# Attention in a four-layer block: probabilities times V in pairs of heads that write opposite halves of the output partitions

## The chip, the cores and the metric

One core of a Trainium2 chip runs the whole program as one launch. The metric is the device time of one execution in microseconds (us), the median of several runs. Five engines work from queues of their own and meet at semaphores: TensorE (PE in the profile, with its weight loads as PEld), VectorE (DVE), ScalarE (ACT), GpSimd (POOL) and SyncE (SP), which issues most transfers.

## The reference, cut to what matters

The program is a block of four layers: a state-space layer, an attention network of depth 2 (attention and a gated feed-forward part, twice), a linear-attention layer and a mixture of experts. The change touches only the local attention, which runs twice (layer 0 and layer 1 below), on 8192 tokens of width 256, 8 heads of 64, windows of 128 tokens, each attending to itself and the window in front of it:

```
def local_attention(q, k, v):              # b, heads 8, n 2048, head width 64
    w = n // WINDOW                        # WINDOW = 128
    bq, bk, bv = windows of q * 8, k, v    # (b, h, w, 128, 64)
    bk, bv = (look_around(bk), look_around(bv))   # window before + own: 256 keys
    sim = jnp.einsum('bhwid,bhwjd->bhwij', bq, bk)
    sim = jnp.where(mask, -jnp.finfo(sim.dtype).max, sim)
    attn = jax.nn.softmax(sim, axis=-1)
    out = jnp.einsum('bhwij,bhwjd->bhwid', attn, bv)      # <- the changed product
    return out.reshape(b, h, n, d)
```

Queries and keys are normalised and rotated first; the output goes through a projection `wo` and is added to the layer's input. All of it is float32.

## The kernel before, in words

`attention()` builds the programs of the five engines for one layer (`made` is true for layer 0, whose queries and keys an earlier stage has already computed; layer 1 computes its own). It walks over 64 tiles of 128 tokens, one window each, and the loops of the engines are written out by hand: the order of calls in a loop is the order in the engine's queue, and semaphores (`wait_ge`, `then_inc`) order the engines among each other. The 8 heads of a tile are worked on in two halves of four, A (half 0) and B (half 1). Per tile and half:

- `scores` (L945) multiplies queries by keys into the PSUM tile `p_s`. A head has only 64 rows, so it takes one half of TensorE's rows; the inner loop over `g` issues two heads on opposite row halves one after the other.
- `maxima` on VectorE (L1151) adds the mask, writes `probA` or `probB` and, per head, the negated maximum into `nb`; ScalarE (L1055) takes the exponential; VectorE divides (`normalise`, L1134 reciprocal, L1138).
- `turn_prob` transposes the probabilities on TensorE (L962) into `p_t`; ScalarE (L1066) and VectorE (L1169) each copy half of it to `probT`.
- `weighted_values` (L975) is the product with V, into the PSUM tile `p_o`, transposed: head `h` takes 64 partitions (the lower half for even `h`, the upper half for odd `h`) and 128 columns. Its keys are two windows, `w` = 0 and 1, from `v` of the tile before and of this one, so each head is two matmuls that accumulate. It uses all 128 rows of TensorE but only 64 of its columns; the start partition of the output says which 64.
- When both halves are done, ScalarE copies `p_o` to `oT` (L1041), TensorE projects (L984), VectorE adds the residual (L1161).

Beside that, per tile, later tiles are prepared: queries and keys are rotated (VectorE L1181, L1184, L1186; GpSimd L1263), their norms are taken (ScalarE L1085, VectorE L1194 and L1196, GpSimd L1259, a power), keys are scaled (GpSimd L1274), both are transposed (TensorE L927, ScalarE L1072), and the values are computed (TensorE L913; in layer 1 also queries and keys, L905).

The order of the calls for one tile `t` of layer 0, which sets what is queued behind what:

- TensorE: scores A, transposing a later input (L895), product with V of half B of tile t-1, scores B (waits for all four maxima of half A), values, transposing A, projection of t-1, transposing the rotated queries and keys of t+1, product with V of half A, transposing B (waits for the copy `qkT` by ScalarE, since both use `p_t`).
- VectorE: maxima A, norms (L1194, L1196), normalise A, maxima B, copy A, residual of t-1 (waits for the projection), normalise B, rotation, copy B.

In layer 1 the order is: on TensorE scores A, L895, product B of t-1, scores B, projection, first part of L905, transposing A, second part, L927, L913, product A, transposing B; on VectorE copy B of t-1, maxima A, normalise A, maxima B, residual, copy A, normalise B, rotation, norms.

The product is issued head by head. `head_at(half, j)` is `4 * half + 2 * (j % 2) + j // 2`, so that `j` = 0, 1 are the two even heads of the half (lower output partitions) and `j` = 2, 3 the two odd ones (upper). A float32 matmul of the program is two MATMUL instructions in the profile, so one group of the product, the work of one half of one tile, is 16 MATMULs. There are 2 halves x 64 tiles x 2 layers = 256 groups.

Of the kernel before, what the change touches and what calls it, by code (L numbers as in the profile page):

```python
# [14 lines left out]
P = 128  # L15
# [9 lines left out]
H, DK = 8, 64  # L25
# [836 lines left out]
def attention(nc, ctx, A, rows, l, ident, identb, mhalf, qk_d, S, before):  # L862
# [7 lines left out]
    qsc, rc, rsn, qkT, vv, prob, probT, nb, den, rden, oT = (  # L870
        S.qsc, S.rc, S.rsn, S.qkT, S.vv, S.prob, S.probT, S.nb, S.den, S.rden, S.oT)
    p_qk, p_v, p_s, p_t, p_o = S.p_qk, S.p_v, S.p_s, S.p_t, S.p_o
# [13 lines left out]
    def head_at(half, j):  # L886
        return 4 * half + 2 * (j % 2) + j // 2

    def tensor(pe, then):
# [75 lines left out]
        def weighted_values(t, half):  # L965
            if half == 0:
                pe.wait_ge(s_ve, n0 + t + 1)
                if t > 0:
                    pe.wait_ge(s_xo, n0 + t)
            pe.wait_ge(s_pe[half], n0 + t + 1)  # L970
            pe.wait_ge(s_pa[half], n0 + t + 1)
            for j in range(4):
                h = head_at(half, j)
                for w, u in enumerate(((t - 1) % RING, t % RING)):
                    ins = pe.matmul(p_o[(h % 2) * DK:(h % 2 + 1) * DK, (h // 2) * P:(h // 2 + 1) * P],  # L975
                                    vv[u][:, h * DK:(h + 1) * DK], probT[:, j, w, :], start=(w == 0), stop=(w == 1),
                                    skip_group_check=True)
            ins.then_inc(s_pv[half], 1)

        def project(t, part):  # L980
# [9 lines left out]
        for t in range(-2, NT + 1):  # L990
# [7 lines left out]
            if t >= 1:  # L998
                weighted_values(t - 1, 1)
# [30 lines left out]
            if now:  # L1030
                weighted_values(t, 0)
                turn_prob(t, 1)
# [1809 lines left out]
```

## Time and profile before

| | |
|---|---|
| median of 3 runs | 5740.58 us (5739.33 to 5742.49) |
| profiled execution, first to last instruction | 5737.1 us |
| PE busy / share of the span | 5081.1 us / 89% |
| DVE | 4318.9 us / 75% |
| ACT | 2963.0 us / 52% |
| POOL | 2975.0 us / 52% |
| L975, the product with V: 4096 MATMULs | 406.0 us busy, 279 ns mean |
| L945, the scores: 4096 MATMULs | 300.7 us busy, 287 ns mean |

The profiled execution is known by its span only; the median lies 3.5 us above it, which is what lies around the first and last instruction. "Busy" is a union: where two instructions of an engine run at once, that time counts once. MATMUL ends are modelled, and each stays on record for some 0.27 us although the next can start earlier, so that an engine with short waits still shows as busy. The layers follow one another: layer 0 runs from about 1947 to 2747 us of the span, layer 1 from about 3240 to 4266 us.

### The profile page before, as it was taken

How to read it: one execution, taken by the hardware profiler on the slowest of the kernel's cores; microseconds unless marked ns; L12 is line 12 of the kernel's file. 1: busy time of each engine (PE TensorE's matmuls, PEld its weight loads, DVE VectorE, ACT ScalarE, POOL GpSimd, SP SyncE). 2: the span in 40 equal slices, each digit the busy share in tenths (PEclk: the TensorE clock that was granted, in tenths of full speed). 3: DMA queues.
4: the chain of work that ended last, by engine and by line, in shares of the span. 5: the costliest groups of instructions: out<-in, count | busy, mean ns of one | idle time of the engine just before them, and what ended most of it. 6: DMA issues, size and time to landing. Idle time of an engine off the chain costs nothing. (4 is left out here: it accounts for less than half of the span.)

```text
span 5737.1 us, 79616 instructions
## 1 busy us (share of the span) xinstructions
PE 5081.1 (89%) x26068; PEld 3035.9 (53%) x26068; DVE 4318.9 (75%) x8753; ACT 2963.0 (52%) x6267; POOL 2975.0 (52%) x1603
## 2 busy tenths in 40 slices
PE   7778777777875699999999999999999999998876
PEld 2223232223221477777655666666665556666765
DVE  3999999999999688888333577777763338994279
ACT  4776776777776477777111355555541114442232
POOL 4999899989989555555111344444431110003733
PEclk9899999989997799999999999999999999999987
DMA  5665556655655222223112111111111134445755
GB/s 134 145 153 144 136 141 153 149 135 146 150 138 120 69 89 84 87 89 95 45 55 73 35 34 34 34 34 34 45 40 55 55 113 141 149 149 137 185 157 178
DMA packets 501470, 593.79 MB, mean 103 GB/s; under 512 B 59702, under 2 KB 380996, under 8 KB 496964
## 3 DMA queue, kind: packets, MB, share of 16 engines
q1 hardware_dynamic: 486756, 579.36, 36.9%
q10 hardware_dynamic: 2016, 7.34, 0.4%
q0 software_dynamic: 12288, 2.00, 0.3%
q8 instruction: 211, 3.46, 0.3%
q14 instruction: 199, 1.63, 0.1%
HBM read 425.05 MB, written 180.37 MB: 106 GB/s over the span
## 5 line engine op out<-in xcount | busy, mean ns | idle before, releaser
L654 POOL TENSOR_TENSOR db<-durep,brep 128x2048 f32<-128x2048 f32 x256 | 1160.5, 4533 | 188.1 <-DVE p_h L561 177.3
L513 ACT ACTIVATE p_h<-dlrep,am 128x512 f32<-128x512 f32 x1024 | 704.5, 691 | 195.8 <-DVE hh L572 170.7
L561 DVE TENSOR_TENSOR_SCAN p_h<-p_h,hlast,db 128x512 f32<-128x512 f32 x576 | 719.9, 1282 | 0.0
L1259 POOL TENSOR_TENSOR rn<-n,mhalf 128x16 f32<-128x16 f32 x128 | 374.9, 2929 | 642.8 <-DVE n L1196 642.7
L349 PE MATMUL p_acc<-hh,fold 128*32 128x512 f32 x2048 | 314.6, 690 | 341.9 <-DVE hh L572 340.7
L572 DVE TENSOR_TENSOR hh<-p_h,crep 128x512 f32<-128x512 f32 x768 | 519.6, 677 | 0.0
L1263 POOL TENSOR_TENSOR rot_cos<-rot_cos,rot_sin 128x1024 f32<-128x1024 f32 x128 | 301.9, 2358 | 220.9 <-DVE rot_sin L1186 220.9
L1635 POOL TENSOR_TENSOR grstd<-grstd,mhalf 128x4 f32<-128x4 f32 x32 | 32.6, 1018 | 737.6 <-DVE grstd L1552 737.5
L975 PE MATMUL p_o<-probT,v 128*64 128x128 f32 x4096 | 406.0, 279 | 6.0 <-DVE probT L1169 3.4
L1066 ACT ACTIVATE probT<-p_t 128x512 f32<-128x512 f32 x256 | 152.8, 597 | 482.0 <-PE p_t L962 482.0
L975 PEld LDWEIGHTS p_o<-probT,v 128*64 128x64 f32 x4096 | 344.1, 137 | 90.4 <-issue 70.6
L1537 ACT ACTIVATE gg<-p_s,b 128x512 f32<-128x512 f32 x160 | 109.9, 687 | 447.4 <-PE p_o L1480 266.2
L349 PEld LDWEIGHTS p_acc<-hh,fold 128*32 128x32 f32 x2048 | 42.4, 114 | 559.9 <-DVE hh L572 535.4
L642 POOL TENSOR_TENSOR hh<-hs,crep 128x512 f32<-128x512 f32 x256 | 327.0, 1277 | 12.6 <-DVE hs L561 12.6
L945 PE MATMUL p_s<-qkT 64*128 64x128 f32 x4096 | 300.7, 287 | 15.8 <-DVE nb L1151 8.0
L1480 PE MATMUL p_s<-ghT,w 128*128 128x512 f32 x640 | 302.5, 595 | 5.2 <-DVE ghid L1589 3.6
L945 PEld LDWEIGHTS p_s<-qkT 64*128 64x128 f32 x4096 | 251.3, 189 | 68.9 <-DVE nb L1151 45.5
L1501 PE MATMUL p_t<-w,ghid 128*128 128x256 f32 x1280 | 284.8, 382 | 0.0
L561 DVE TENSOR_TENSOR_SCAN hs<-p_h,hlast,db 128x512 f32<-128x512 f32 x192 | 245.5, 1279 | 49.1 <-ACT p_h L513 46.8
L1055 ACT ACTIVATE probB<-probB,nb 128x256 f32<-128x256 f32 x512 | 253.3, 498 | 50.3 <-DVE nb L1151 50.3
L227 PE MATMUL p_f<-mxT,w_in 128*128 128x512 f32 x512 | 259.8, 654 | 8.1 <-ACT mxT L390 5.5
L502 ACT ACTIVATE hlast<-p_h 128x1 f32<-128x1 f32 x576 | 95.3, 166 | 329.9 <-DVE hh L572 328.8
(285 smaller groups left out, 11994.9 us busy)
## 6 DMA issues: line engine op xcount, KB each, us to landing
dlrep<-delta_rows SPq DMA_DIRECT2D x256, 256.0 KB
durep<-drive_rows SPq DMA_DIRECT2D x256, 256.0 KB
ew<-in_L_ffn_w SPq DMA_DIRECT2D x192, 176.0 KB
first_queries_keys<-qs SPq DMA_DIRECT2D x128, 256.0 KB, 2.1
qk<-first_queries_keys SPq DMA_DIRECT2D x64, 512.0 KB, 3.8
brep<-bc_rows SPq DMA_DIRECT2D x64, 256.0 KB
crep<-bc_rows SPq DMA_DIRECT2D x64, 256.0 KB
delta_rows<-dl SPq DMA_DIRECT2D x64, 256.0 KB
```

The lines of the kernel that those rows point to most:

```text
L349: ins = pe.matmul(p_acc[32 * j:32 * j + 32, :], fold[:], hh[s % 2][:, j], start=False, stop=(g == NG - 1), skip_group_check=True)
L513: act.activation(p_h[:, (i % BANKS) * CH:(i % BANKS + 1) * CH], dlrep[use % 2][:, j], ACT.Exp, scale=am[:, q, j, g:g + 1]).then_inc(s_ex, 1)
L561: dve.tensor_tensor_scan(out=state, data0=bank, data1=db[s % 2][:, j], initial=0.0 if first else hlast[:, i % TILES:i % TILES + 1], op0=AL ...
L572: dve.tensor_tensor(out=hh[s % 2][:, j], in0=p_h[:, (i % BANKS) * CH:(i % BANKS + 1) * CH], in1=crep[c % 2][:, s % NG], op=ALU.mult).then_ ...
L642: pool.tensor_tensor(out=hh[s % 2][:, 0], in0=hs[s % 2][:], in1=crep[c % 2][:, s % NG], op=ALU.mult).then_inc(s_hp, 1)
L654: pool.tensor_tensor(out=db[s % 2][:], in0=durep[use % 2][:], in1=brep[c % 2][:, g:g + 1, :].to_broadcast([P, 4, CH]), op=ALU.mult).then_i ...
L945: ins = pe.matmul(p_s[:, at:at + P], here[g * DK:(g + 1) * DK, c:c + P], there[g * DK:(g + 1) * DK, INNER + c:INNER + c + P], start=True, ...
L975: ins = pe.matmul(p_o[(h % 2) * DK:(h % 2 + 1) * DK, (h // 2) * P:(h // 2 + 1) * P], vv[u][:, h * DK:(h + 1) * DK], probT[:, j, w, :], sta ...
L1259: pool.tensor_tensor(out=rn[f % 2][:], in0=n2[f % 2][:], in1=mhalf[:], op=ALU.pow).then_inc(s_rn, 1)
L1263: pool.tensor_tensor(out=rc[:], in0=rc[:], in1=rsn[:], op=ALU.add).then_inc(s_rot, 1)
L1480: ins = pe.matmul(dst[:], w1[:, f, o + j * P:o + (j + 1) * P], hT[:, f, :], start=(f == 0), stop=(f == DH - 1))
L1501: ins = pe.matmul(p_y[:, j0 * D:(j0 + 1) * D], hid[:, j, j0 * P:(j0 + 1) * P], w2[:, j, :], start=False, stop=(j == FB - 1), skip_group_ch ...
```

## The change

The four heads of a group are no longer issued one after the other. The outer loop now goes over `a` (which of the two 128-column blocks of `p_o`), then over the two windows `w`, and the inner loop over `g`, the lower and the upper half of the output partitions. So a matmul for the lower half is followed by one for the upper half. The number, the shapes, the operands and the semaphores of the group stay, and so does its place in the queue.

```diff
-            for j in range(4):
-                h = head_at(half, j)
+            for a in range(2):
                 for w, u in enumerate(((t - 1) % RING, t % RING)):
-                    ins = pe.matmul(p_o[(h % 2) * DK:(h % 2 + 1) * DK, (h // 2) * P:(h // 2 + 1) * P],
-                                    vv[u][:, h * DK:(h + 1) * DK], probT[:, j, w, :], start=(w == 0), stop=(w == 1),
-                                    skip_group_check=True)
+                    for g in range(2):
+                        j, h = 2 * g + a, 4 * half + 2 * a + g
+                        ins = pe.matmul(p_o[g * DK:(g + 1) * DK, (h // 2) * P:(h // 2 + 1) * P],
+                                        vv[u][:, h * DK:(h + 1) * DK], probT[:, j, w, :], start=(w == 0), stop=(w == 1),
+                                        skip_group_check=True)
             ins.then_inc(s_pv[half], 1)
```

TensorE's queue in layer 0, the first tile, half A, before. Here `v3` and `v0` are the values of the window before and of the tile's own; each row is one matmul of the program, in the order lower, lower, lower, lower, upper, upper, upper, upper half of the output:

```order
L927 MATMUL p_t<-ident,rot_cos 128x128 x8
L975 MATMUL p_o<-probT,v3 64x128
L975 MATMUL p_o<-probT,v0 64x128
L975 MATMUL p_o<-probT,v3 64x128
L975 MATMUL p_o<-probT,v0 64x128
L975 MATMUL p_o<-probT,v3 64x128
L975 MATMUL p_o<-probT,v0 64x128
L975 MATMUL p_o<-probT,v3 64x128
L975 MATMUL p_o<-probT,v0 64x128
L962 MATMUL p_t<-ident,probB 128x128 x8
```

The same place now; "x2" is a lower and an upper half with the same V tile:

```order
L927 MATMUL p_t<-ident,rot_cos 128x128 x8
L976 MATMUL p_o<-probT,v3 64x128 x2
L976 MATMUL p_o<-probT,v0 64x128 x2
L976 MATMUL p_o<-probT,v3 64x128 x2
L976 MATMUL p_o<-probT,v0 64x128 x2
L962 MATMUL p_t<-ident,probB 128x128 x8
```

The eight matmuls are the same ones in another order, and the transposes around them have not moved.

Half B of the same tile, in front of the scores B of the next one, as it stands now:

```order
L895 MATMUL p_v<-ident,hx1 128x128 x2
L976 MATMUL p_o<-probT,v3 64x128 x2
L976 MATMUL p_o<-probT,v0 64x128 x2
L976 MATMUL p_o<-probT,v3 64x128 x2
L976 MATMUL p_o<-probT,v0 64x128 x2
L945 MATMUL p_s<-qkT0,qkT1 128x128 x2
```

Again only the order inside the group is new. The other engines' queues are unchanged.

## Rows read from the trace of the kernel before

**Rows 1.** Busy time by stretch: length, each engine's busy us (instructions), clock, DMA.
```profile
2100.00:2300.00 200.00, 198.55 (x1662) 154.78 (x1661) 179.20 (x554) 151.84 (x394) 117.36 (x82) 1.00 0.29 86
3800.00:4000.00 200.00, 197.32 (x1396) 136.31 (x1394) 158.70 (x424) 107.69 (x287) 92.06 (x62) 1.00 0.11 34
4200.00:4240.00 40.00, 37.23 (x267) 25.60 (x265) 32.88 (x89) 20.48 (x52) 16.54 (x10) 1.00 0.08 24
```

**Rows 2.** Timeline, TensorE, a tile of layer 0: start, length, engine, line, count.
```profile
2402.85 1.06 PE L927 MATMUL p_t<-ident,rot_cos 128*128 128x128 f32 x8
2403.84 1.58 PE L975 MATMUL p_o<-probT,v 128*64 128x128 f32 x16
2405.35 1.09 PE L962 MATMUL p_t<-ident,probB 128*128 128x128 f32 x8
2406.38 1.16 PE L945 MATMUL p_s<-qkT 64*128 64x128 f32 x16
...
2407.84 1.58 PE L975 MATMUL p_o<-probT,v 128*64 128x128 f32 x16
2409.49 1.16 PE L945 MATMUL p_s<-qkT 64*128 64x128 f32 x16
...
2413.27 1.89 PE L984 MATMUL p_o<-wo,oT 128*128 128x256 f32 x8
```

**Rows 3.** Timeline, VectorE, the same tile; idle time before and releaser in brackets.
```profile
2397.02 0.08 DVE L1151 DVE_READ_ACCUMULATOR2_ANT nb<- 128x1 f32 x1
...
2402.97 0.43 DVE L1161 TENSOR_TENSOR xo<-p_o,res 128x256 f32<-128x256 f32 x1 [1.05 <-PE p_o L984]
...
2406.90 0.68 DVE L1169 COPY probT<-p_t 128x512 f32<-128x512 f32 x1
2407.72 0.48 DVE L1151 CUSTOM_DVE_ANT_0 probA<-p_s,msk,qsc 128x256 f32<-128x256 f32 x1
...
2409.35 0.08 DVE L1151 DVE_READ_ACCUMULATOR2_ANT nb<- 128x1 f32 x1
```

**Rows 4.** Timeline, ScalarE, the same tile: the copy of queries and keys.
```profile
2404.01 1.03 ACT L1072 ACTIVATE qkT<-p_t 128x1024 f32<-128x1024 f32 x1 [1.24 <-PE p_t L927]
```

**Rows 5.** Groups by line, VectorE, 1971 to 2711 us (60 tiles of layer 0).
```profile
L1151 DVE CUSTOM_DVE_ANT_0 probA<-p_s,msk,qsc 128x256 f32<-128x256 f32 x240 | 102.1, 481 | 9.4 <-PE p_s L945 2.4
```

**Rows 6.** Timeline, VectorE, the one tile of layer 0 where TensorE came early.
```profile
2230.33 0.43 DVE L1161 TENSOR_TENSOR xo<-p_o,res 128x256 f32<-128x256 f32 x1 [0.86 <-PE p_o L984]
...
2234.26 0.69 DVE L1169 COPY probT<-p_t 128x512 f32<-128x512 f32 x1
2234.93 0.48 DVE L1151 CUSTOM_DVE_ANT_0 probA<-p_s,msk,qsc 128x256 f32<-128x256 f32 x1
...
2242.50 0.43 DVE L1161 TENSOR_TENSOR xo<-p_o,res 128x256 f32<-128x256 f32 x1 [1.05 <-PE p_o L984]
```

**Rows 7.** Timeline, VectorE, a tile of layer 1.
```profile
3852.22 0.69 DVE L1169 COPY probT<-p_t 128x512 f32<-128x512 f32 x1
3852.83 0.47 DVE L1151 CUSTOM_DVE_ANT_0 probA<-p_s,msk,qsc 128x256 f32<-128x256 f32 x1
...
3856.53 2.85 DVE L1138 TENSOR_SCALAR probA<-probA,rden 128x256 f32<-128x256 f32 x4
...
3863.55 1.14 DVE L1138 TENSOR_SCALAR probB<-probB,rden 128x256 f32<-128x256 f32 x4
```

**Rows 8.** Timeline, GpSimd, the same tile of layer 1.
```profile
3852.39 2.93 POOL L1259 TENSOR_TENSOR rn<-n,mhalf 128x16 f32<-128x16 f32 x1 [8.48 <-DVE n L1196]
3855.29 2.35 POOL L1263 TENSOR_TENSOR rot_cos<-rot_cos,rot_sin 128x1024 f32<-128x1024 f32 x1
...
3858.18 1.04 POOL L1274 TENSOR_TENSOR rot_cos<-rot_cos,rn 128x512 f32<-128x512 f32 x1
...
3868.44 2.93 POOL L1259 TENSOR_TENSOR rn<-n,mhalf 128x16 f32<-128x16 f32 x1 [8.47 <-DVE n L1196]
```

**Rows 9.** Timeline, TensorE, the same tile of layer 1: transposing half A.
```profile
3859.52 1.06 PE L962 MATMUL p_t<-ident,probA 128*128 128x128 f32 x8
```

## The prediction

> **What bounds the kernel now.** I read the busy time by stretch first, for one stretch of each attention layer [rows 1]. TensorE is busy 198.6 of 200 us in layer 0 and 197.3 of 200 in layer 1, VectorE 179.2 and 158.7. By these shares TensorE is the bound, and a shorter product with V would be gained in full. The share is not proof, though: a MATMUL stays on record 0.27 us, longer than most of TensorE's waits. So I went on to the timeline of one tile and followed every start back to what released it.
>
> A group of the product is 16 MATMULs in 1.58 us [rows 2]. Eight transposes behind it take 1.09, of which the last one's record is 0.27, so sixteen one behind the other would be 2 x (1.09 - 0.27) + 0.27 = 1.91. The group is already 0.33 shorter than that, three steps of about 0.11: where the lower half's last heads meet the upper half's first ones, the two halves run at once. Scores, whose two heads take opposite row halves in turn, need 1.16 for the same 16 [rows 2].
>
> **What the change does to the group.** With lower and upper halves in turn, both streams can start together. Each has 8 MATMULs, so the group should take what 8 take, 1.09, at best, and 1.16 if it behaves as the scores do. That is 0.42 to 0.49 us off each group; I take 0.45, and the result below hardly depends on it. Nothing is added: same instructions, loads and semaphores. If TensorE were the bound, 256 x 0.45 = 115 us would go. What the tile's cycle gives back is less.
>
> At this point a rule speaks against the change. The Trainium skill (TensorE: Matmul & The Clock Gate, Part 3, "The mechanism") says that a weight load overlaps matmuls in flight only when its row group differs; both halves here use all 128 rows, so by that rule the pairs would run one behind the other. The trace has 16 in 1.58 and not in 1.91 [rows 2], with all rows in use in every one, so it does not agree. What the rule would make of the time is the slower rival below.
>
> **Layer 0, the cycle of one tile.** Let M be the moment at which the four maxima of half A are done: 2397.10, and again 2409.43, so a tile takes 12.33 [rows 3]. I follow it around once:
>
> - M to the residual on VectorE, 2397.10 to 2402.97 = 5.87. TensorE starts scores B 0.06 behind M (2409.43 to 2409.49 [rows 2, 3]), then come values, transposing A and the projection without a gap, and VectorE waits 1.05 for the projection [rows 3]. No product with V is in this stretch.
> - Residual to the first maximum, 2402.97 to 2407.72 = 4.75: normalise B, rotation, copy B, all on VectorE.
> - First maximum to M, 2407.72 to 2409.43 = 1.71.
>
> The sum is 12.33, the tile. The group of half B (2407.84) lies beside the maxima and ends in front of M; shortened, TensorE only waits longer for M at scores B. It gives nothing. The group of half A (2403.84) lies beside the middle stretch, and there it matters a little: copy B ends at 2406.90 + 0.68 = 2407.58, but the first maximum starts only at 2407.72, 0.14 later [rows 3]. In layer 1, where the scores are there in time, the same two instructions overlap by 0.08 (3852.22 + 0.69 = 3852.91 against 3852.83 [rows 7]). So VectorE loses 0.22 per tile, and it waits for scores A, which end at 2406.38 + 1.16 = 2407.54. The group by line agrees: 9.4 us idle before the 60 tiles' maxima, 0.16 each [rows 5].
>
> One tile shows what happens when scores A come early. There the projection had been late against everything else, and the first maximum started at 2234.93, 0.02 in front of the copy's end; that tile took 2242.50 - 2230.33 = 12.17 instead of 12.33 [rows 6]. The gap shrank by 0.16 and the tile by 0.16.
>
> How early can scores A be? Transposing B stands in front of them and waits for two things: TensorE itself, behind the group of half A, and ScalarE's copy of `qkT`, since both use `p_t`. The copy ends at 2404.01 + 1.03 = 2405.04 [rows 4], so with 0.06 for the semaphore, as at scores B, transposing B can start at 2405.10 instead of 2405.35 [rows 2]. The group of half A would be over by 2405.35 - 0.42 = 2404.93 at the latest: the copy, and no longer the group, is what is late next. So 0.25 is opened of the 0.42 to 0.49, and VectorE can use 0.22.
>
> The new tile, two ways around. By VectorE: 5.87 + (4.75 - 0.22) + 1.71 = 12.11. By TensorE and ScalarE: M to L927 (2397.10 to 2402.85) 5.75, to the copy's start 1.16, copy 1.03, semaphore 0.06, transposing B to scores A 1.03, scores A to the maximum (2406.38 to 2407.72) 1.34, maxima 1.71, together 12.08. The longer one holds: 12.11, so 0.22 off a tile. Bounds: 0.22 where VectorE's natural step is as in layer 1; 0.16 where it is only as in the early tile; nothing if the copy reaches TensorE 0.2 later than I think. I take 0.22 for 60 tiles: 13.2 us. The first and last tiles have other waits and I leave them out.
>
> **Layer 1.** A tile takes 16.05 (3852.39 to 3868.44 [rows 8]). Around: VectorE's norms release GpSimd's power (3852.39, 2.93), then the addition L1263 (3855.29 to 3857.64) and, behind a short one, L1274 (3858.18 to 3859.22). Normalise A starts on VectorE at 3856.53 and takes 2.85 for four instructions; normalise B, the same four without GpSimd beside them, takes 1.14. It ends at 3859.38, 0.16 behind L1274 [rows 7, 8]. So VectorE is held while GpSimd's two additions run. Then transposing A (3859.52 [rows 9]), its copies, the exponentials B, normalise B, the rotation and the norms follow without a gap and close the cycle. Neither group of the product is in it. Group B shortened lets ScalarE copy `oT` earlier, by 0.45 at most, and with it the exponentials A, but normalise A would then be ready at 3856.08 instead of 3856.53, still inside L1263. So layer 1 gives 0 in 64 tiles. Bounds: 0, and 0.45 x 64 = 29 us if that hold does not stand.
>
> **The ends.** Where a layer hands over to the gated part, TensorE works without waits, and there I count two groups at 0.45, 0.9 us.
>
> **The sum.** 13.2 + 0 + 0.9 = 14.1. The profiled execution's span of 5737.1 becomes 5723.0; the median of the runs lies 3.5 above its span (5740.6), which makes 5726.5.
>
> **The rivals.**
>
> No change (0 to 6 us off). The gap of 0.14 is VectorE's own and not a wait, or transposing B does not start when `qkT` is there, or the pairs run together no better than now. For it: the view of waits names scores A for only 2.4 of the 9.4 us [rows 5]. Against it: the early tile [rows 6] and the overlap in layer 1 [rows 7]. About 5739.
>
> More than forecast. If TensorE is the bound in spite of all this, all 115 us go: 5626. For it stand the shares [rows 1]. Against it: VectorE cannot do a tile of layer 0 in less than its work, 179.2/200 x 12.33 = 11.05, so no more than 1.28 a tile could go in any case, and the cycle names a wait at each place. The milder form has the 29 us of layer 1, or a part of them, on top: 5698.
>
> Slower. The two halves cannot load and compute in turn, and the group falls back to sixteen steps, 1.91 instead of 1.58. In layer 0 the group of half A holds transposing B, so each tile grows by 0.33: 64 x 0.33 = 21 us. In layer 1 TensorE's own work per tile grows by 2 x 0.33 = 0.66, of which the idle time it shows, (200 - 197.3) / 200 x 16.05 = 0.22, covers a third: 0.44 x 64 = 28. Together 49: 5790. It decides from a group longer than 1.58. Against it is the overlap that is there already [rows 2]. A fall of the granted clock because TensorE waits more is a smaller case: in the stretch 4200 to 4240 TensorE was busy 93% at clock 1.00 [rows 1], and with 0.9 off 12.33 of work in a tile of 12.11 I expect about 94% in layer 0. Half the clock for one whole tile would cost up to 6 us, so it decides from three such tiles.
>
> **How the numbers follow.** Forecast 0.67, no change 0.17, more 0.10, slower 0.06. Within the forecast the gain is 8 to 18 us. A measurement can tell about 0.2% from no change, 11.5 us, and the forecast of 14.1 lies just past it: four fifths of its chance are faster, one fifth is same. Faster: 0.54 + 0.09 = 0.63. Same: 0.13 + 0.17 + 0.01 = 0.31. Slower 0.06. The range takes in the forecast, the no-change case and half of the mild form of more: 5712 to 5741; about 0.14 is outside.
>
> **What would show it.** Right: a group of L976 in 1.09 to 1.16; in layer 0 the first maximum starting 0.08 in front of the copy's end, no idle time before it, transposing B 0.06 behind ScalarE's `qkT`, tiles of 12.11, and TensorE waiting some 0.5 for M at scores B; in layer 1 tiles of 16.05 as before with normalise A at 2.85. Wrong: a group of 1.5 or longer; tiles of 12.33 in layer 0 although the group is short (then another wait stands behind this one); tiles shorter than 12.0, or a change in layer 1.

## The result, and the profile after

The changed kernel takes 5725.35 us (median of 10 runs, 5722.4 to 5729.21), the kernel before 5740.51 (10 runs): 15.2 us less, ratio 0.9974, 95% interval 0.9965 to 0.9983. Forecast were 5726.5 us and 14.1 less.

In the timeline of TensorE for a tile of layer 0 the group (now L976) stands at 1.09 us twice, where [rows 2] have 1.58:

```profile
2397.39 1.06 PE L927 MATMUL p_t<-ident,rot_cos 128*128 128x128 f32 x8
2398.38 1.09 PE L976 MATMUL p_o<-probT,v 128*64 128x128 f32 x16
2399.63 1.09 PE L962 MATMUL p_t<-ident,probB 128*128 128x128 f32 x8 [0.16 <-ACT qkT L1073]
2400.66 1.16 PE L945 MATMUL p_s<-qkT 64*128 64x128 f32 x16
...
2402.17 1.09 PE L976 MATMUL p_o<-probT,v 128*64 128x128 f32 x16
2403.79 1.16 PE L945 MATMUL p_s<-qkT 64*128 64x128 f32 x16 [0.52 <-DVE nb L1152]
...
2407.57 1.89 PE L985 MATMUL p_o<-wo,oT 128*128 128x256 f32 x8
2409.48 1.06 PE L927 MATMUL p_t<-ident,rot_cos 128*128 128x128 f32 x8
```

Both groups are 0.49 shorter, and behind each there is now a wait: transposing B for ScalarE's copy of `qkT` (0.16 on record), scores B for VectorE's maxima (0.52). From L927 to L927 the tile is 2409.48 - 2397.39 = 12.09. The 16 weight loads of the first group lie within 0.85 us, and the copy ends at 2398.55 + 1.03 = 2399.58, 0.05 before transposing B starts:

```profile
2398.38 0.85 PEld L976 LDWEIGHTS p_o<-probT,v 128*64 128x64 f32 x16 [0.17 <-issue]
2398.55 1.03 ACT L1073 ACTIVATE qkT<-p_t 128x1024 f32<-128x1024 f32 x1 [1.24 <-PE p_t L927]
```

VectorE in the same tile, against [rows 3]:

```profile
2397.51 0.42 DVE L1162 TENSOR_TENSOR xo<-p_o,res 128x256 f32<-128x256 f32 x1 [1.03 <-PE p_o L985]
...
2401.44 0.68 DVE L1170 COPY probT<-p_t 128x512 f32<-128x512 f32 x1
2402.03 0.47 DVE L1152 CUSTOM_DVE_ANT_0 probA<-p_s,msk,qsc 128x256 f32<-128x256 f32 x1
...
2403.65 0.08 DVE L1152 DVE_READ_ACCUMULATOR2_ANT nb<- 128x1 f32 x1
...
2409.60 0.42 DVE L1162 TENSOR_TENSOR xo<-p_o,res 128x256 f32<-128x256 f32 x1 [1.03 <-PE p_o L985]
```

The first maximum starts at 2402.03, 0.09 in front of the copy's end (2401.44 + 0.68), where it came 0.14 behind it. The stretches are 4.52 (residual to maximum), 1.70 (to M, 2403.73) and 5.87 (M to the next residual), together 12.09. The group by line for 60 tiles of layer 0, against [rows 5]: 0.2 us idle where there were 9.4.

```profile
L1152 DVE CUSTOM_DVE_ANT_0 probA<-p_s,msk,qsc 128x256 f32<-128x256 f32 x240 | 101.6, 480 | 0.2 <-issue 0.2
```

The busy time by stretch, against the first two rows of [rows 1]:

```profile
2100.00:2300.00 200.00, 188.13 (x1678) 141.39 (x1675) 181.38 (x566) 155.32 (x404) 121.24 (x83) 1.00 0.28 86
3800.00:4000.00 200.00, 185.34 (x1380) 123.58 (x1380) 161.28 (x421) 106.90 (x287) 89.72 (x61) 1.00 0.12 35
```

TensorE is 10 and 12 us less busy in 200, the granted clock stays at 1.00 in both stretches, and only layer 0 got faster. In layer 1 normalise A is held as before, here by a little more than in [rows 7]. The first line is the reciprocal in front of it in the kernel before, the other two are from the changed kernel:

```profile
3856.32 0.18 DVE L1134 RECIPROCAL rden<-den 128x4 f32<-128x4 f32 x1 [1.79 <-ACT probA L1055]
...
3858.40 0.18 DVE L1135 RECIPROCAL rden<-den 128x4 f32<-128x4 f32 x1 [1.54 <-ACT probA L1056]
3858.61 3.11 DVE L1139 TENSOR_SCALAR probA<-probA,rden 128x256 f32<-128x256 f32 x4
```

It is ready earlier (VectorE waits 1.54 instead of 1.79) and takes as much longer (3.11 instead of 2.85). Where the time went, by the starts of VectorE's residuals in the two profiled executions: 60 tiles of layer 0 take 726.5 us instead of 741.0 (14.5 less), the stretch from there to layer 1's first residual 552.9 instead of 555.1 (2.2 less), 60 tiles of layer 1 963.0 instead of 962.8, the rest 1506.1 instead of 1507.1 (1.0 less); layer 0 starts 2.9 later, behind a stage that the change does not touch. The sum, 14.5 + 2.2 - 0.2 + 1.0 - 2.9, is 14.6, the difference of the spans.

Nearly all of the 2.2 falls in the last three steps between residuals of layer 0, behind the 60 tiles: 16.47 + 12.56 + 9.12 = 38.15 instead of 16.36 + 14.14 + 9.60 = 40.10. There the granted clock fell twice in the kernel before, and only once in the changed one. In the second fall transposing A took 1.65 us and the projection 3.03; the changed kernel has 1.07 and 1.89 there, and 14.14 - 12.56 = 1.6 for the step. The first line is the place of the second fall in the kernel before, the other is everything behind the one fall in the changed kernel:

```profile
2738.00:2742.00 4.00, 4.00 (x15) 3.50 (x16) 2.11 (x9) 2.67 (x9) 0.00 (x0) 0.57 0.00 0
...
2718.00:2738.00 20.00, 15.67 (x147) 12.20 (x148) 11.39 (x39) 9.51 (x24) 0.00 (x0) 1.00 0.08 21
```

### The profile page after: what moved, and what is told of

Read it like the earlier page. It is cut to its first block and busy times, and to the rows that moved or that the text cites. A ratio compares the mean times of both kernels' runs of the same rounds, so it can differ in the third digit from the quotient of the medians.

```text
span 5722.5 us, 79616 instructions
## 1 busy us (share of the span) xinstructions
PE 4973.4 (87%) x26068; PEld 2915.5 (51%) x26068; DVE 4329.7 (76%) x8753; ACT 2959.3 (52%) x6267; POOL 2977.6 (52%) x1603
## 5 line engine op out<-in xcount | busy, mean ns | idle before, releaser
L976 PE MATMUL p_o<-probT,v 128*64 128x128 f32 x4096 | 281.0, 279 | 36.9 <-DVE probT L1170 36.7
L976 PEld LDWEIGHTS p_o<-probT,v 128*64 128x64 f32 x4096 | 219.1, 137 | 125.4 <-DVE probT L1170 64.4
L1056 ACT ACTIVATE probA<-probA,nb 128x256 f32<-128x256 f32 x512 | 253.2, 496 | 39.6 <-DVE nb L1152 39.6
L1139 DVE TENSOR_SCALAR probA<-probA,rden 128x256 f32<-128x256 f32 x512 | 268.3, 586 | 4.9 <-DVE rden L1135 0.4
```

Source lines behind the costliest of these rows:

```text
L976: ins = pe.matmul(p_o[g * DK:(g + 1) * DK, (h // 2) * P:(h // 2 + 1) * P], vv[u][:, h * DK:(h + 1) * DK], probT[:, j, w, :], start=(w == 0 ...
L1056: ins = act.activation(prob[half][:, j], prob[half][:, j], ACT.Exp, bias=nb[:, h:h + 1], scale=-1.0, accum_out=den[t % 2][:, h:h + 1])
```

## The experiments

All were timed against the kernel before on the same chip; its median was 5738.04 us beside e1 to e4, 5738.50 beside p1 to p4, and 5740.45 beside e5, p5, p6 and p7. "Tile" is the median step from one of VectorE's residuals to the next, over 60 tiles of each layer. In layer 1 of e3_half_work and p1_pool_pairs the steps differ from tile to tile, and their mean is 17.06 in both.

| kernel | median us | against before: ratio (95%) | tile, layer 0 | tile, layer 1 |
|---|---|---|---|---|
| before | 5740.51 | | 12.33 | 16.05 |
| changed | 5725.35 | 0.9974 (0.9965 to 0.9983) | 12.10 | 16.05 |
| e1_half_a | 5723.97 | 0.9976 (0.9966 to 0.9986) | 12.09 | 16.04 |
| e2_half_b | 5738.76 | 1.0000 (0.9991 to 1.0009) | 12.33 | 16.05 |
| e3_half_work | 5782.22 | 1.0077 (1.0064 to 1.0091) | 12.09 | 17.23 |
| e4_norm_two | 5719.47 | 0.9969 (0.9957 to 0.9981) | 12.07 | 16.05 |
| e5_half_work_fill | 5724.85 | 0.9973 (0.9963 to 0.9983) | 12.10 | 16.05 |
| p1_pool_pairs | 5786.96 | 1.0087 (1.0073 to 1.0100) | 12.10 | 16.84 |
| p2_pool_heads | 5785.03 | 1.0083 (1.0069 to 1.0097) | 12.33 | 16.84 |
| p7_pool_pairs_fill | 5777.19 | 1.0063 (1.0049 to 1.0077) | 12.10 | 16.85 |
| p3_turn_first_pairs | 5764.64 | 1.0046 (1.0032 to 1.0059) | 12.10 | 16.72 |
| p4_turn_first_heads | 5783.12 | 1.0078 (1.0065 to 1.0092) | 12.33 | 16.73 |
| p5_norms_first_pairs | 5706.85 | 0.9938 (0.9925 to 0.9952) | 12.10 | 15.74 |
| p6_norms_first_heads | 5722.23 | 0.9966 (0.9954 to 0.9979) | 12.33 | 15.75 |

**Which of the two groups counts.** The edit of both kernels, with `half == 0` in the first and `half == 1` in the second:

```diff
-            for j in range(4):
-                h = head_at(half, j)
-                for w, u in enumerate(((t - 1) % RING, t % RING)):
+            paired = [(2 * g + a, w) for a in range(2) for w in range(2) for g in range(2)]
+            by_head = [(j, w) for j in range(4) for w in range(2)]
+            for j, w in (paired if half == 0 else by_head):
...
```

> The lower and upper heads in turn in the groups of half A alone; half B keeps the order head by head. The theory of the cycle: in layer 0 only the group of half A lies between the transposed queries and keys and the first maximum, so this gives all that the full change gives, tiles of 12.10 us in layer 0 and 16.05 in layer 1, 13 to 15 us off the kernel before. Rival (each shortened group counts alike, in whatever part TensorE is the bound): half of the full change, 7 to 8 us off and tiles of 12.21 in layer 0.

> The lower and upper heads in turn in the groups of half B alone. The theory of the cycle: TensorE then waits for the maxima at scores B by so much longer, some 0.6 us instead of 0.1; tiles of 12.33 us in layer 0 and 16.05 in layer 1, 0 to 1 us off the kernel before. Rival (each shortened group counts alike): 7 to 8 us off and tiles of 12.21 in layer 0.

Half A alone gives 14.1 us (5723.97 against 5738.04), all of the change; half B alone gives nothing. Busy time in 200 us of layer 0, first with half A, then with half B alone:

```profile
2100.00:2300.00 200.00, 196.57 (x1676) 149.51 (x1675) 180.58 (x565) 154.14 (x396) 121.00 (x84) 1.00 0.29 86
```

```profile
2100.00:2300.00 200.00, 190.86 (x1648) 146.97 (x1647) 179.15 (x555) 151.12 (x391) 118.86 (x82) 1.00 0.28 86
```

The kernel in which TensorE is busy 196.6 us is the fast one. Per tile TensorE is busy nearly alike in the two, 196.57/200 x 12.09 = 11.9 us and 190.86/200 x 12.33 = 11.8, against 198.55/200 x 12.33 = 12.2 before. With half B alone the saved time becomes a wait of some 0.5 us for the maxima, which half A alone doesn't have. TensorE's waits in the same 200 us (total, times, longest), first with half A, then with half B alone:

```profile
PE p_t L962 <- ACT qkT L1073: 2.4, 15, 0.2
```

```profile
PE p_s L945 <- DVE nb L1152: 8.9, 16, 0.6
```

**What holds the tile now.** One kernel makes the group still shorter, by leaving the window before out of the product (each matmul left then has `start` and `stop` both true), the other makes VectorE's stretch shorter. Both are edits of the changed kernel.

```diff
-                for w, u in enumerate(((t - 1) % RING, t % RING)):
+                for w, u in ((1, t % RING),):                          # e3_half_work
...
-            for j in range(4):
+            for j in (range(2) if made and half == 1 else range(4)):   # e4_norm_two, in normalise
```

> The changed kernel with only half of the product: the matmuls for the window before (w = 0) are left out, so each group is 8 MATMULs instead of 16 and about 0.65 us instead of 1.09. The theory of the cycle: once the group is shorter than ScalarE's copy of qkT the copy and VectorE hold the tile, so nothing more is gained in the tiles, 12.10 us in layer 0 and 16.05 in layer 1; against the changed kernel 0 to 2 us off, at the ends of the layers. Rival (the group itself still holds the tile, TensorE being the bound): 0.4 us per group, 25 us off for one group per tile of layer 0 and up to 110 for all.

> The changed kernel, in which VectorE's normalise B of layer 0 treats only two of the four heads (the other two keep undivided probabilities), so that its stretch from the residual to the first maximum is 0.52 us shorter. The theory of the cycle: the way over TensorE and ScalarE (transposed queries and keys, their copy, transposing B, scores A) is only 0.02 to 0.03 us shorter than VectorE's, so tiles of layer 0 go from 12.10 to 12.07 us, 1 to 2 us off the changed kernel, and VectorE again waits for scores A, some 0.5 us. Rival (VectorE alone holds the tile, the way over the copy has slack): 0.5 us per tile, 30 us off.

e4_norm_two came out as expected: 12.07, and the group of maxima waits for scores A again, 24.0 us over 60 tiles, 0.4 each. VectorE's stretch had 0.52 taken out and 0.03 came of it.

```profile
L1152 DVE CUSTOM_DVE_ANT_0 probA<-p_s,msk,qsc 128x256 f32<-128x256 f32 x240 | 101.9, 480 | 24.0 <-PE p_s L945 23.9
```

In layer 0 e3_half_work did as expected too: 12.09. In layer 1 it was slower with less to do, by 1.2 us a tile in the median and 1.0 in the mean (60 tiles took 1023.8 us instead of 963.0), which no theory had. Its timeline of TensorE there:

```profile
3851.32 0.44 PE L895 MATMUL p_v<-ident,hx 128*128 128x128 f32 x2
3852.80 0.66 PE L976 MATMUL p_o<-probT,v 128*64 128x128 f32 x8 [1.04 <-DVE probT L1170]
3854.41 1.77 PE L945 MATMUL p_s<-qkT 64*128 64x128 f32 x16 [0.95 <-DVE nb L1152]
3856.12 3.00 PE L985 MATMUL p_o<-wo,oT 128*128 128x256 f32 x8
```

Scores B take 1.77 instead of 1.16 and the projection 3.00 instead of 1.99 ([rows 2] have 1.16 and 1.89 in layer 0): behind two waits of about 1 us, with 0.66 of work between them, the clock fell. The granted clock is 1.00 before it, 0.50 in the projection, which is the level of 1.2 GHz, and 1.00 again 3 us later:

```profile
3852.50:3854.40 1.90, 0.66 (x8) 0.42 (x8) 1.86 (x9) 1.16 (x5) 1.90 (x1) 1.00 0.00 0
3856.00:3857.00 1.00, 1.00 (x4) 0.79 (x3) 0.96 (x2) 0.00 (x0) 1.00 (x1) 0.50 0.03 8
3859.00:3860.00 1.00, 1.00 (x4) 0.52 (x3) 1.00 (x6) 0.00 (x0) 0.79 (x2) 1.00 0.00 0
```

Over a longer stretch it is 0.92:

```profile
3800.00:4000.00 200.00, 175.67 (x1107) 118.49 (x1104) 152.64 (x401) 98.67 (x272) 88.87 (x60) 0.92 0.10 30
```

**Was it the clock?** In e3_half_work the wait in front of the group is filled with work that changes nothing: the two transposes of the input (L895) are issued five times.

```diff
-            for c in range(DH):
+            for c in list(range(DH)) * (1 if made else 5):
                 ins = pe.transpose(p_v[:, c * P:(c + 1) * P], hx[f % 2][:, c * P:(c + 1) * P], ident[:])
```

> As e3_half_work (the products with the window before left out), with four repeats of the two transposes of the input (L895) in layer 1, 8 MATMULs or 0.87 us more, in the place where TensorE waited 1.1 us there for VectorE's copy B. They write the same values again and change nothing else. e3_half_work had tiles of about 17.3 us in layer 1 at a mean granted clock of 0.92, the changed kernel 16.05 at 1.00. Theory: the long waits made TensorE's clock fall once in most tiles, and that alone made the tile longer; with the wait filled the clock stays at 1.00 and the tile is back at 16.05, 75 to 80 us faster than e3_half_work though TensorE has more to do, within 2 us of the changed kernel. Rival (something else in the shorter group made layer 1 longer): 17.3 us as before, or more.

```profile
3854.15 1.31 PE L895 MATMUL p_v<-ident,hx 128*128 128x128 f32 x10
3855.56 0.66 PE L976 MATMUL p_o<-probT,v 128*64 128x128 f32 x8
3857.17 1.16 PE L945 MATMUL p_s<-qkT 64*128 64x128 f32 x16 [0.96 <-DVE nb L1152]
```

```profile
3800.00:4000.00 200.00, 185.47 (x1280) 123.81 (x1278) 161.28 (x421) 106.75 (x288) 89.45 (x61) 1.00 0.12 35
```

With 8 MATMULs more per tile layer 1 is back at 16.05 and clock 1.00 (60 tiles in 963.0 us), and the kernel 57 us faster than e3_half_work (the medians of two sets). So the fall of the clock was the whole of the loss. The 75 to 80 us that were expected are too many: they take the 17.3 of a typical tile of e3_half_work for all, where the mean is 17.06. The run also settles that the group's length, 16 or 8 MATMULs, plays no part in either layer once the pairs are there: 5724.85, as the changed kernel.

**Layer 1's bound.** If GpSimd's addition (L1263) is what holds normalise A, moving it should show. First by the order of GpSimd's own queue:

```diff
-                inverse_norm(f)
                 add_halves(f)
+                inverse_norm(f)
                 query_scale(f)
```

> The changed kernel with one edit in layer 1: GpSimd adds the two halves of the rotation before it takes the power for the norms (as it does in layer 0), so that the addition no longer holds VectorE's normalise A. The theory of the cycle, which has layer 1 run over the norms, GpSimd and normalise A: normalise A ends about 1 us earlier, transposing A then waits for TensorE instead (it would start 4.70 us behind the maxima A instead of 5.00), so tiles of 15.74 us in layer 1 instead of 16.05 and 19 to 20 us off the changed kernel, about 5705; normalise A takes well under 2.85 us. Rival (TensorE or ScalarE hold layer 1 at 16.05): no difference to the changed kernel.

> The same edit of GpSimd's order in layer 1, with the product head by head as in the kernel before. The theory of the cycle: the group of half A still ends in front of VectorE's rotation and norms (scores A would allow the first maximum 9.26 us behind transposing A, VectorE reaches it at 9.35), so tiles of 15.74 in layer 1 here too and 12.33 in layer 0, 20 us off the kernel before; the pairs are then worth the same 15 us as without this edit. Rival (with GpSimd out of the way TensorE is the bound in layer 1): the pairs are worth up to 1 us per tile, 60 us, so this kernel gains little or nothing and p1_pool_pairs much more.

Both expectations were wrong: 48 and 47 us slower than before. VectorE and GpSimd in p1_pool_pairs:

```profile
3854.84 1.21 DVE L1195 TENSOR_REDUCE n<-sq 128x16 f32<-128x1024 f32 x1
3856.08 1.30 DVE L1197 TENSOR_SCALAR n<-n 128x16 f32<-128x16 f32 x1
3857.30 0.68 DVE L1170 COPY probT<-p_t 128x512 f32<-128x512 f32 x1
...
3861.34 1.98 DVE L1139 TENSOR_SCALAR probA<-probA,rden 128x256 f32<-128x256 f32 x4
```

```profile
3855.00 2.35 POOL L1264 TENSOR_TENSOR rot_cos<-rot_cos,rot_sin 128x1024 f32<-128x1024 f32 x1 [10.24 <-DVE rot_sin L1187]
```

Normalise A did get shorter (1.98), but the addition now met the clamp of the norms (L1196, now L1197, which keeps them above a small floor), an instruction of 16 elements per partition that otherwise takes 0.17 us and here 1.30, until the addition's end at 3857.35. The cycle of layer 1 runs through it. So GpSimd's hold on VectorE was there as supposed, and I had not gone through every instruction of VectorE that it could meet. Here the pairs also cost time in layer 1: 60 tiles took 1023.5 us with them and 1009.8 without, since the wait in front of group B is longer and the clock falls (mean 0.97 in 3800 to 4000, against 1.00). The same filling tests it:

> As p1_pool_pairs, with the same 8 repeated MATMULs in layer 1, where TensorE waited 1.8 us for the copy B. p1_pool_pairs had 17.06 us per tile in layer 1 at clock 0.97, p2_pool_heads 16.83 at 1.00. Theory (the pairs lengthen a wait, and the clock falls): with the fill the clock falls seldom or not at all and the tile is 16.80 to 16.85, 13 to 15 us off p1_pool_pairs. Rival (the pairs cost time in layer 1 in another way): 17.06 or more.

60 tiles of layer 1 went back to 1010.3 us, 13.2 less, and the clock in 3800 to 4000 to 1.00. The kernel went from 48.5 above before to 36.7 above, 11.7 less by these two differences and 9.8 by the two medians, a little under the 13 to 15 expected.

Two kernels were meant to put the group into layer 1's cycle, by transposing A before both parts of L905:

```diff
+                if now:
+                    turn_prob(t, 0)
                 if f < NT:
                     queries_keys(f, 0)
-                if now:
-                    turn_prob(t, 0)
-                if f < NT:
                     queries_keys(f, 1)
```

> As p1_pool_pairs, and in layer 1 TensorE transposes the probabilities A before, not between, the two parts of the queries and keys. Made so that the product with V lies in the cycle of layer 1: transposing A comes about 1 us earlier against the maxima, but both parts of L905 are then behind it, and scores A come late, about 10.5 us behind transposing A. The theory of the cycle: tiles of about 15.9 us in layer 1, 5 to 10 us slower than p1_pool_pairs, and VectorE waits for scores A. Rival (transposing A early is what counts): tiles of 15.0 to 15.4, 25 to 45 us faster than p1_pool_pairs.

> As p3_turn_first_pairs, with the product head by head. Here the theory of the cycle has the group of half A in the cycle of layer 1 with its full length: tiles about 0.49 us longer than in p3_turn_first_pairs (some 16.4 us), 31 us more in layer 1 beside the 15 us of layer 0, together 45 us between the two. Rival (the pairs are worth the same anywhere, or nothing in layer 1): 15 us between the two.

Both expectations were wrong: 15.9 and about 16.4 us a tile were expected, and the tiles of layer 1 are alike, 16.72 and 16.73. The held clamp (1.31 in both) makes VectorE later than scores A in both. The 18.5 us between the two are mostly those of layer 0 and its end (13.7 and 2.4 in the profiled pair, 0.6 in layer 1). Against p1_pool_pairs, p3_turn_first_pairs is 22 us faster where 5 to 10 slower was expected; its clock is 1.00 in 3800 to 4000 where p1_pool_pairs has 0.97. A case in which the pairs shorten a tile of layer 1 was not found.

**Out of the addition's way.** The other way to move it: the norms before the rotation, on VectorE.

```diff
                 if f < NT:
-                    rotate(f)
                     square_sums(f)
+                    rotate(f)
```

> The changed kernel with one edit in layer 1: VectorE takes the norms (L1194, L1196) before the rotation instead of behind it, so that GpSimd's power, addition and scaling all come 1.3 us earlier against normalise A, and no instruction of the norms meets GpSimd's addition (in p1_pool_pairs that held L1196 for 1.1 us). The theory of the cycle: normalise A ends about 1.2 us earlier, transposing A then waits for TensorE, tiles of 15.74 us in layer 1, 19 to 20 us off the changed kernel, about 5705. Rival (another instruction is held in turn, or the clock falls in the waits): 16.05 or more.

> The same edit with the product head by head. The theory of the cycle: tiles of 15.74 us in layer 1 and 12.33 in layer 0, about 15 us slower than p5_norms_first_pairs, as between the kernel before and the changed one. Rival (with tiles this short TensorE is the bound in layer 1): tiles of up to 16.0 in layer 1, 15 us more between the two.

VectorE and GpSimd in p5_norms_first_pairs:

```profile
3852.51 0.17 DVE L1197 TENSOR_SCALAR n<-n 128x16 f32<-128x16 f32 x1
...
3859.18 1.71 DVE L1139 TENSOR_SCALAR probA<-probA,rden 128x256 f32<-128x256 f32 x4 [0.21 <-DVE rden L1135]
```

```profile
3855.66 2.36 POOL L1264 TENSOR_TENSOR rot_cos<-rot_cos,rot_sin 128x1024 f32<-128x1024 f32 x1
```

The clamp is at 0.17, normalise A at 1.71, the tile at 15.74, the number that was worked out, and the kernel at 5706.85 us, 33.6 below before and the fastest of all. The addition is over at 3858.02, before normalise A starts; that normalise A still takes more than 1.14 goes with GpSimd's scaling of the keys, which runs beside it (L1275, 3858.43 to 3859.47). Between p5 and p6 lie 15.4 us: the pairs are worth the same with and without this edit, for they act in layer 0 alone.

## Why the prediction was right

- The group: 1.09 at best was forecast, and 1.09 is what it takes, 0.49 less. The two halves load and compute at once although both use all rows. So the rule of the Trainium skill that was weighed (TensorE: Matmul & The Clock Gate, Part 3, "The mechanism") does not agree with this trace, and the slower rival worked out beside it, a group of 1.91, is refuted.
- TensorE's busy share is not the bound. Shown by e1 and e2: of two groups shortened alike one is worth all, the other nothing.
- The 0.22 per tile: measured 12.33 to 12.10, 0.23. It needed two rows, the gap in front of the first maximum and the natural overlap of the same two instructions in layer 1. The 60 tiles gave 14.5 us where 13.2 were forecast: 0.23 for 0.22 makes half of the difference. The rest comes from the few longer tiles, which together lay 1.2 above 60 x 12.33 before and lie 0.5 above 60 x 12.10 now; why was not followed.
- The two ways around, 12.11 and 12.08: e4 shortened the first and the tile stopped at 12.07, so the second is real and as close as worked out. The copy of `qkT` is what is late next (transposing B starts 0.05 behind it).
- Layer 1 at 0: measured 16.05 before and after. The hold by GpSimd was shown from both sides by p1 (the addition meets another instruction, slower) and p5 (it meets none that it holds, 0.31 off a tile). The prediction calls what holds normalise A "GpSimd's two additions"; the second (L1274) is the scaling of the keys.
- The ends: this term was right in sign only. 0.9 was forecast, for two shorter groups. The last three steps of layer 0 alone gave 2.0, most of it by the granted clock, which the prediction did not look at there: the second fall of the kernel before is gone. It is not the chance of one execution: the four other kernels with half A head by head have the two falls and 39.6 to 40.1 us for these steps; e1, p1, p3, p5 and p7 have one fall and 37.8 to 38.6. (e4 and e5, which differ in more, have a second fall again, and 38.2 and 38.1 us; so the fall is not the whole of the difference in every kernel.) The 1.0 behind layer 1 can't be told from chance: the start of layer 0 moved by 2.9 in an untouched stage.
- The closeness of the total is in part luck. In the profiled pair everything from layer 0 on gave 17.5 (14.5 + 2.2 - 0.2 + 1.0), and the late start of layer 0 took 2.9 back; e1, with half A alone, measured 14.1 by its medians, and the pair p5 and p6 15.4. Also, the 3.5 us added to the span are not all what lies around the first and last instruction: each run's time is only some 1.7 above its own span, and the rest is the distance of one profiled execution from the median. The changed kernel's median lies 2.85 above its profiled span (5725.35 - 5722.5). This cancels in the 14.1, not in the 5726.5.
- The clock in the tiles: TensorE busy 94% in layer 0 was forecast and found, with no fall in the 60 tiles of either layer. The rival of a falling clock was real all the same: e3, with two waits of about 1 us in a tile where the changed kernel has 0.45 and 0.52, had a mean of 0.92 in layer 1, and e5, with that wait filled, 1.00.

## What to carry to other kernels

A busy share near 100% does not say that an engine is the bound; follow one period of the loop, and a saving counts only where the saved stretch is on the longest way around, and only until the next way. Two rows decide its size: the gap that the wait leaves now, and the same pair of instructions somewhere without the wait. And where an instruction of one engine is held by another engine's, list every instruction that the holder could meet in the new order before moving it. Where a saving turns into a wait of TensorE, look at the granted clock too: it took more here (44 us in e3) than the whole change had gained.

## What the runs showed of the hardware

- Matmuls of 64 output columns on opposite halves of the output partitions run as pairs, 16 in 1.09 us, with their weight loads, while each uses all 128 rows. Issued eight and eight, the same 16 take 1.58; 1.09 is what 8 transposes of 128x128 take.
- Less work on TensorE can make a kernel slower: e3 lost 44 us against before by a mean granted clock of 0.92 in layer 1, and e5 won it back with 8 repeated MATMULs per tile. The projection in a lowered stretch (granted clock 0.50, the level of 1.2 GHz) took 3.00 us, at 1.00 (2.4 GHz) 1.99.
- A change worth 0.23 us a tile gained 2.0 us in the last three steps of layer 0, where a fall of the granted clock (0.57 in 2738 to 2742 before) did not come.
- A GpSimd addition of 128x1024 (2.35 us) held VectorE's TENSOR_SCALAR instructions: four of 128x256 in layer 1 (1.14 us became 2.85 and 3.11, with GpSimd's scaling beside their end) and one of 128x16 (0.17 became 1.30). It did not hold the reduction L1195 beside it in p1 (1.21 us, as without it), nor, in layer 0 of the changed kernel, the copy out of PSUM that starts at 2401.44 (0.68, as without it). GpSimd's power of 128x16 (2.93 us) did not hold even the four TENSOR_SCALAR of normalise A, which take 1.14 beside it there:

```profile
2401.61 2.37 POOL L1264 TENSOR_TENSOR rot_cos<-rot_cos,rot_sin 128x1024 f32<-128x1024 f32 x1 [3.42 <-DVE rot_sin L1187]
...
2405.15 2.93 POOL L1260 TENSOR_TENSOR rn<-n,mhalf 128x16 f32<-128x16 f32 x1 [1.18 <-DVE n L1197]
...
2405.21 1.14 DVE L1139 TENSOR_SCALAR probA<-probA,rden 128x256 f32<-128x256 f32 x4
```
